# Gated cross-attention and mixture of experts on one core: the routing table built from four single-pass columns per tile instead of two fp32 ones

## The chip, the cores and the metric

One core of a Trainium2 chip runs the whole kernel in one launch. The metric is device time in microseconds (us), from the start to the end of the execution. TensorE does matrix products, VectorE, ScalarE and GpSimd work on rows of up to 128 partitions, SyncE issues DMAs. In rows of the profile PE is TensorE, PEld its weight loads, DVE is VectorE, ACT is ScalarE, POOL is GpSimd, SP is SyncE.

## The reference, cut to what matters

```python
x = x + tanh(g_xattn) * attention(layernorm(x), ctx)        # 32 heads, 8 groups, causal
xt = layernorm(x).reshape(2048, 512)                         # T = 2048 tokens
scores = softmax(xt @ Wg.T)                                  # E = 16 experts
masked = scores of the 2 best of 4 groups of experts, -inf elsewhere
topi = top_k(masked, 4);  weights = scores at topi
combine = zeros(T, E).at[token, topi].add(weights)
y = sum over experts e of (silu(xt @ W1[e].T) * (xt @ W3[e].T)) @ W2[e].T * combine[:, e]
z = (silu(xt @ Ws1.T) * (xt @ Ws3.T)) @ Ws2.T                # the shared expert
x = x + tanh(g_ffn) * (y + z)
```

## The kernel before, in words

`build` runs five stages: `stage_project`, `stage_attend`, `stage_close`, `stage_shared` and `stage_experts`. The change lies in `stage_shared` alone, which computes the shared expert and, woven into it, the routing. `stage_experts` follows and works through TILES = 79 tiles of 128 gathered rows, each of one expert.

**The shared expert.** The work is cut into 24 units, `units`, in the order b = 0 to 3 (512 tokens each) and, within b, n = 5, 0, 1, 2, 3, 4 (128 hidden columns each, the first only 64). A unit is 12 products for `gate` and 12 for `up` (`multiply`, L1405; unit n = 5 has only `gate`). Each is an fp32r product, that is one pass over fp32 words that hold a rounded value; three such passes over a high and a low part (`PASSES`) make up fp32. After the last unit of a b come 68 products into `yps` (`down`, L1417). Behind each unit ScalarE takes `act` and `upc` out of PSUM, GpSimd multiplies them into `raw` (L1378), ScalarE rounds that to the high part of `h` (L1340), and GpSimd subtracts it to get the low part (L1380). `gate` and `up` have two buffers each, so that TensorE in unit i waits for ScalarE's work on unit i - 2 (`s_act`, `s_upc`).

**Routing.** VectorE alone works out the softmax, the four experts of each token, and for each of the 2048 x 4 pairs of token and expert a slot in the list of 79 x 128 rows: `row` (slot mod 128) and `col` (slot div 128), for NT = 16 groups of 128 tokens and NK = 4 choices. Its small operations wait for each other by the semaphore `s_v`, one after the other. It waits once on TensorE for the counts (L1198).

**The table.** What the experts stage needs is the inverse: for each slot, which token is in it and at which scale. It is made as a sum of outer products. For each group t VectorE writes `at_row[t % 2]` (L1250: 1 where `row` equals the partition number, [128, 4, 128], 512 elements per partition), `at_tile` (L1254: 1 where `col` equals the tile number, [128, 4, 79], one buffer), and `at_col[t % 2]` (L1258, twice: `at_tile` times `put[..., 0]`, which is the token's number less T less `row`, and `at_tile` times `put[..., 1]`, the scale; [128, 4, 79] each). TensorE then runs `table(t)` (L1427): for each k one fp32 product of `at_row[:, k]` (128x128, as weights) and `at_col[:, k]` (158 columns), all 64 of them summed in the PSUM tile `tokps` [128, 158].

**The order around it.** TensorE runs its queue in order. After the products of unit i, for i = 8 to 15, it runs `table(2 * (i - 8))` and `table(2 * (i - 8) + 1)`, each behind a wait on `s_row` for VectorE's operations of that group. Units 8 to 11 are followed by the `down` products of b = 1, and units 12 to 15 are the first of b = 2 (unit 12 is the narrow one). VectorE, before it writes `at_row` of group t, waits on `s_tok` for `table(t - 2)`; nothing else holds it in this loop. After the tables VectorE turns `tokps` into `scatter`, `gather` and `scale` (L1284 to L1293). GpSimd waits for `gather` (`compared[1]`) before unit 20 of 24, where it issues the first four gathers, and the experts stage reads `scatter` and `scale`.

```python
for k in range(NK):
    mm = eng.matmul(tokps[:], at_row[r][:, k, :], at_col[r][:, k].rearrange("p n g -> p (n g)"), start=t == 0 and k == 0,
```

Of the kernel before, what the change touches and what calls it, by code (L numbers as in the profile page):

```python
# [9 lines left out]
F32 = mybir.dt.float32  # L10
F32R = mybir.dt.float32r
# [5 lines left out]
P = 128  # L17
BATCH, SEQ, D = 4, 512, 512
T = BATCH * SEQ
# [11 lines left out]
E, EG, TOPG, TOPK = 16, 4, 2, 4  # L31
# [4 lines left out]
NT = T // P  # L36
TILES = T * TOPK // P + E - 1
# [1021 lines left out]
def stage_shared(nc, io, dram, out):  # L1059

    with ExitStack() as c:  # L1061
        sb = lambda n, s, d=F32: c.enter_context(nc.sbuf_tensor(n, s, d))
        sem = dsem = lambda n: c.enter_context(nc.semaphore(n))

        NG, NK, SEAM = E // EG, TOPK, 24
        big = lambda n, d=F32: sb(n, [P, NT, E], d)
# [4 lines left out]
        top, topi, topf = sb("r_top", [P, NT, 8]), sb("r_topi", [P, NT, 8], mybir.dt.uint32), sb("r_topf", [P, NT, 8])  # L1071
# [8 lines left out]
        tok, slots = sb("r_tok", [P, NT]), sb("r_slots", [P, NT, NK], I32)  # L1080
# [3 lines left out]
        row, col = sb("r_row", [P, NT, NK]), sb("r_col", [P, NT, NK])  # L1084
        at_row = [io["rows"][2 + r].rearrange("p (k n) -> p k n", k=NK) for r in range(2)]
        at_tile = sb("r_attile", [P, NK, TILES])
        at_col = [sb(f"r_atcol{r}", [P, NK, 2, TILES]) for r in range(2)]
        put = sb("r_put", [P, NT, NK, 2])
        pad_i, pad = sb("r_padi", [P, 1], I32), sb("r_pad", [P, 1])
# [6 lines left out]
        within, totals = counts[:, 0], counts[:, 1]  # L1096
        tokps = ps("r_tokps", [P, 2 * TILES])
        s_c, s_i, s_exp, s_ch, s_mm, s_v = (
# [9 lines left out]
        x1 = [residual(io, b) for b in range(BATCH)]  # L1108
        gf, tg = sb("s_gf", [P, 1]), sb("s_tg", [P, 1])
        gate = [ps(f"s_gate{i}", [P, SEQ]) for i in range(2)]  # L1110
        up = [ps(f"s_up{i}", [P, SEQ]) for i in range(2)]
# [11 lines left out]
        def _(eng):  # L1123
            begin(eng, s_c, s_ch, s_v, s_row, s_tile, s_high, s_low)
            done = itertools.count(2)
            eng.wait_ge(s_i, 6)
            eng.tensor_copy(pad[:], pad_i[:]).then_inc(s_v, 1)
            eng.wait_ge(s_v, next(done))
            eng.tensor_copy(iota_e[:], iota_i[:]).then_inc(s_v, 1)
# [54 lines left out]
            eng.wait_ge(s_tg, 2)  # L1184
            eng.tensor_scalar(put[:, :, :, 1], top[:, :, 0:NK], tg[:, 0:1], None, ALU.mult).then_inc(s_v, 1)
            eng.wait_ge(s_v, next(done))
# [56 lines left out]
            eng.wait_ge(s_v, next(done))  # L1243
            eng.tensor_tensor(put[:, :, :, 0], rows(tok[:].rearrange("p (t o) -> p t o", o=1), NK), row[:], ALU.subtract).then_inc(s_v, 1)
            eng.wait_ge(s_v, next(done))
            for t in range(NT):
                r = t % 2
                if t >= 2:
                    eng.wait_ge(s_tok, t)
                eng.tensor_tensor(at_row[r], iota_p[:].rearrange("p (o n) -> p o n", o=1).broadcast_to([P, NK, P]),  # L1250
                                  row[:, t, :].rearrange("p (k o) -> p k o", o=1).broadcast_to([P, NK, P]), ALU.is_equal).then_inc(s_row, 1)
                if t:
                    eng.wait_ge(s_row, 3 * t + 1)
                eng.tensor_tensor(at_tile[:], iota_g[:].rearrange("p (o g) -> p o g", o=1).broadcast_to([P, NK, TILES]),  # L1254
                                  col[:, t, :].rearrange("p (k o) -> p k o", o=1).broadcast_to([P, NK, TILES]), ALU.is_equal).then_inc(s_tile, 1)
                eng.wait_ge(s_tile, t + 2)
                for n in range(2):
                    eng.tensor_tensor(at_col[r][:, :, n, :], at_tile[:],  # L1258
                                      put[:, t, :, n:n + 1].broadcast_to([P, NK, TILES]), ALU.mult).then_inc(s_row, 1)

# [23 lines left out]
            eng.tensor_scalar(indexf[:], tokps[:, 0:TILES], pad[:, 0:1], None, ALU.add).then_inc(s_v, 1)  # L1284
            eng.wait_ge(s_v, next(done))
            eng.tensor_copy(io["scatter"], indexf[:]).then_inc(s_v, 1)
            eng.wait_ge(s_v, next(done))
# [4 lines left out]
            eng.wait_ge(s_v, compared[1])  # L1292
            eng.tensor_copy(io["scale"], tokps[:, TILES:]).then_inc(s_v, 1)  # L1293
            eng.wait_ge(s_v, next(done))
# [57 lines left out]
        def _(eng):  # L1352
            begin(eng, s_i, s_xlow, s_raw, s_hlow, s_sum)
            eng.iota(iota_i[:], pattern=[[1, E]], base=0, channel_multiplier=0).then_inc(s_i, 1)
            eng.iota(tok_i[:], pattern=[[P, NT]], base=-T, channel_multiplier=1).then_inc(s_i, 1)
            eng.iota(iotag_i[:], pattern=[[1, TILES]], base=0, channel_multiplier=0).then_inc(s_i, 1)
# [32 lines left out]
        def _(eng):  # L1389
# [33 lines left out]
            def table(t):  # L1423
                r = t % 2
                eng.wait_ge(s_row, 3 * t + 4)
                for k in range(NK):
                    mm = eng.matmul(tokps[:], at_row[r][:, k, :], at_col[r][:, k].rearrange("p n g -> p (n g)"), start=t == 0 and k == 0,  # L1427
                                    stop=t == NT - 1 and k == NK - 1, skip_group_check=True)
                mm.then_inc(s_tok, 1)
# [386 lines left out]
```

## Time and profile before

| | |
|---|---|
| median of 3 runs | 1238.58 us |
| lowest, highest | 1228.62, 1242.21 us |
| the profiled execution, its own time | 1229.68 us |
| its span, first to last instruction | 1227.9 us |
| mean granted TensorE clock | 0.985 |
| busy: PE, PEld | 1190.7 us (97%), 917.2 us (75%) |
| busy: DVE, ACT, POOL | 631.8 us (51%), 576.0 us (47%), 618.1 us (50%) |

The profiled execution is near the lowest of the three runs. Its time is 1.8 us more than its span. The stage with the change runs from about 440 to 660 us of the span, the tables from 517 to 586 us. Start times in the rows are in us from the span's start. A line of a timeline with x12 at its end is 12 instructions in a row, with the time from the start of the first to the end of the last; the ends of matmuls overlap the next ones, so the distance between two starts is what one costs its engine.

### The profile page before, as it was taken

What the parts mean: (1) busy time and instruction counts of PE and PEld (TensorE: products, weight loads), DVE (VectorE), ACT (ScalarE), POOL (GpSimd) and SP (SyncE); (2) the same over time, 40 slices, a digit from 0 to 9 for tenths busy, and PEclk for the clock granted to TensorE, in tenths of its full rate; (3) what the DMA queues carried; (4) which work ended last, traced back from release to release, by engine and by line L of the source; (5) the groups of instructions that cost most, each with busy time, mean ns of one, the idle gap of its engine ahead of it and who ended that gap; (6) DMA issues with size and microseconds to landing.
All of it is one profiled execution on the core that took longest, in us unless ns stands there. A gap on an engine that the chain in (4) does not pass through costs nothing. (4 is left out here: it accounts for less than half of the span.)

```text
span 1227.9 us, 23555 instructions
## 1 busy us (share of the span) xinstructions
PE 1190.7 (97%) x7779; PEld 917.2 (75%) x7780; DVE 631.8 (51%) x1829; ACT 576.0 (47%) x989; POOL 618.1 (50%) x655
## 2 busy tenths in 40 slices
PE   7999999999988989999998999999999999999996
PEld 5564555555543468888887999999999999999995
DVE  5437999999947847865141233222423344442100
ACT  1221777777741333322332555555555555555553
POOL 5010333443332615635562766667666676666663
PEclk8999999999989989999999999999999999999998
DMA  9462544444449250110133546566565655656433
GB/s 351 150 192 99 155 127 124 133 128 129 147 132 256 85 206 32 38 38 32 52 123 114 116 101 146 142 147 146 147 144 122 169 146 147 147 147 144 73 69 43
DMA packets 74829, 157.73 MB, mean 128 GB/s; under 512 B 10836, under 2 KB 16468, under 8 KB 73608
## 3 DMA queue, kind: packets, MB, share of 16 engines
q1 hardware_dynamic: 53720, 106.96, 27.1%
q0 software_dynamic: 21040, 49.88, 19.8%
q8 instruction: 41, 0.67, 0.2%
q14 instruction: 28, 0.23, 0.1%
HBM read 101.88 MB, written 52.49 MB: 126 GB/s over the span
## 5 line engine op out<-in xcount | busy, mean ns | idle before, releaser
L1555 DVE CAST e_w<-e_w 128x480 fp32r<-128x480 f32 x135 | 71.5, 530 | 304.9 <-DMA e_w<-in_w2T 300.8
L670 DVE CUSTOM_DVE_ANT_0 a_mb<-a_mb,late 128x512 f32<-128x512 f32 (+1 forms) x480 | 217.3, 526 | 6.4 <-PE a_mb L712 4.6
L1711 PE MATMUL e_yps<-e_w,e_hT 128*128 x711 | 197.2, 404 | 0.9 <-ACT e_hT L1620 0.9
L656 ACT ACTIVATE a_at<-a_eb 128x1024 f32<-128x1024 f32 (+1 forms) x192 | 163.5, 870 | 38.3 <-PE a_eb L733 25.7
L1582 POOL DMA_INDIRECT out<-e_y,scatter x79 | 130.4, 1651 | 99.0 <-ACT e_y L1629 95.4
L576 POOL TENSOR_SCALAR_AFFINE_SELECT a_at<-a_at 128x256 f32<-128x256 f32 (+1 forms) x192 | 93.8, 489 | 171.0 <-ACT a_at L656 170.9
L1690 PE MATMUL e_up<-e_w,e_xT 128*128 x948 | 170.5, 329 | 0.0
L1690 PE MATMUL e_gate<-e_w,e_xT 128*128 x948 | 168.8, 327 | 1.0 <-issue 1.0
L1690 PEld LDWEIGHTS e_gate<-e_w,e_xT 128*128 128x128 f32 x948 | 156.8, 190 | 11.1 <-issue 6.3
L1690 PEld LDWEIGHTS e_up<-e_w,e_xT 128*128 128x128 f32 x948 | 149.7, 189 | 0.0
L1711 PEld LDWEIGHTS e_yps<-e_w,e_hT 128*128 128x128 f32 x711 | 128.1, 189 | 25.4 <-issue 1.2
L712 PE MATMUL a_mb<-a_k,a_q 49*128 49x512 f32 (+1 forms) x480 | 132.3, 372 | 0.8 <-PEq L245 0.8
L712 PEld LDWEIGHTS a_mb<-a_k,a_q 49*128 49x128 f32 x480 | 74.2, 184 | 65.5 <-DVE a_mx L670 39.1
L1587 POOL TENSOR_TENSOR e_hT<-e_hc,e_hT 128x384 fp32r<-128x384 f32 x78 | 83.2, 1066 | 44.5 <-ACT e_hc L1622 44.4
L1562 DVE TENSOR_TENSOR e_w<-e_w 128x480 fp32r<-128x480 f32 x135 | 101.1, 749 | 4.7
L756 PE MATMUL a_pv<-a_at,a_v 128*32 128x128 f32 (+1 forms) x1792 | 102.2, 327 | 0.2
L1600 POOL TENSOR_TENSOR e_h<-e_act,e_upc 128x352 f32<-128x352 f32 x79 | 76.3, 966 | 39.7 <-ACT e_upc L1640 39.5
L105 POOL DMA_INDIRECT e_x<-dx,gather x79 | 81.9, 1036 | 12.2 <-issue 2.4
L1616 ACT ACTIVATE e_xT<-e_xps 128x512 fp32r<-128x512 f32 x79 | 47.2, 597 | 81.6 <-PE e_xps L1681 75.4
L733 PE MATMUL a_eb<-a_q,a_k 50*128 50x512 f32 (+1 forms) x256 | 84.2, 420 | 0.1
L1636 ACT ACTIVATE e_act<-e_gate 128x352 f32<-128x352 f32 x79 | 36.8, 465 | 95.1 <-PE e_gate L1690 77.9
L1640 ACT ACTIVATE e_upc<-e_up 128x352 f32<-128x352 f32 x79 | 36.9, 467 | 79.1 <-PE e_up L1690 79.1
(259 smaller groups left out, 1858.3 us busy)
## 6 DMA issues: line engine op xcount, KB each, us to landing
e_w<-in_w13T SPq DMA_DIRECT2D x16, 1408.0 KB, 7.1
dq<-p_parts SPq DMA_DIRECT2D x32, 256.0 KB, 2.4
a_q<-dq SPq DMA_DIRECT2D x64, 128.0 KB
do<-a_o SPq DMA_DIRECT2D x32, 256.0 KB, 2.3
e_w<-in_w2T SPq DMA_DIRECT2D x16, 512.0 KB, 4.2
a_k<-dk SPq DMA_DIRECT2D x64, 98.0 KB
e_w<-in_ctxT SPq DMA_DIRECT2D x4, 1024.0 KB, 15.3
e_w<-in_x SPq DMA_DIRECT2D x4, 1024.0 KB, 13.7
```

What stands on the lines that cost most here:

```text
L105: eng.indirect_dma_start(out=io["rows"][n], out_offset=None, in_=dram["x2"], in_offset=bass.IndirectOffsetOnAxis(ap=io["gather"][:, g:g + ...
L576: eng.affine_select(out=square, in_=square, compare_op=ALU.is_ge, fill=0.0, base=0, pattern=[[0, 2 * len(js)], [1, P]], channel_multiplier ...
L656: eng.activation(to, scores, ACT.Exp, scale=0.25).then_inc(s_exp, 1)
L670: eng.tensor_tensor_reduce(out=b[:, 0:w], in0=b[:, 0:w], in1=io["late"][:, SEQ - w:SEQ], scale=1.0, scalar=3 * NEG, op0=ALU.add, op1=ALU.m ...
L712: mm = eng.matmul(b, q[r][rows, j, ch * P:(ch + 1) * P], k[r][rows, 0:b.shape[-1]], start=True, stop=True)
L733: return eng.matmul(eb[u % 2][:, t, n0:SEQ], keys, q[r][rows, js[0], n0:SEQ], start=True, stop=True)
L756: mm = eng.matmul(pv[32 * h:32 * h + 32, cols], v[of % NB][:, ch, :], at[of % 2][:, ch, 2 * j + t, cols], start=ch == 0 and n0 == 0, stop= ...
L1562: eng.tensor_tensor(w[rows, r, rest], w[rows, r, rest].bitcast(F32), w[rows, r, cols].bitcast(F32), ALU.subtract).then_inc(s_low, 1)
L1582: eng.indirect_dma_start(out=out, out_offset=bass.IndirectOffsetOnAxis(ap=io["scatter"][:, g:g + 1], axis=0), in_=y[n][:], in_offset=None, ...
L1587: eng.tensor_tensor(hT[r][:, 1], hc[:], hT[r][:, 0].bitcast(F32), ALU.subtract).then_inc(s_hlow, 1)
L1690: mm = eng.matmul(out[r][:], xT[r][:, mine, k, :], w[:, bass.ds(buf, 1), its * SIDE + at:its * SIDE + at + INTER].rearrange("p b n -> p (b ...
L1711: mm = eng.matmul(yps[:], hT[r][0:size, mine, n, :], w[0:size, bass.ds(buf, 1), its * SIDE + at:its * SIDE + at + D].rearrange("p b n -> p ...
```

## The change

The table's products become fp32r, one pass each. An fp32r value holds fewer bits than an fp32 one, so index and scale are cut into parts that fp32r holds: a whole number between -127 and 127 (`lane - row`: the token's number within its group less its row), the group's multiple of 128 (`tok`, now without the lane), the scale's rounded part (`high`), and what it leaves. `put` and `at_col` so have PARTS = 4 columns where they had 2, `tokps` has 316 columns, and a product has 316 columns in place of 158. The four are multiplied by one VectorE operation per group, over [128, 4, 4, 79] = 1264 elements per partition, in place of two of 316. Five operations on 64 elements stand where one stood (before the first `at_row`), one of one element per partition is added at the stage's start, and after the tables two additions of 79 elements put the parts together again. The wait counts on `s_row` follow (two increments a group where there were three). Nothing else moves; all queues keep their order.

```diff
@@ -1062,7 +1062,7 @@
         sb = lambda n, s, d=F32: c.enter_context(nc.sbuf_tensor(n, s, d))
         sem = dsem = lambda n: c.enter_context(nc.semaphore(n))
 
-        NG, NK, SEAM = E // EG, TOPK, 24
+        NG, NK, SEAM, PARTS = E // EG, TOPK, 24, 4
         big = lambda n, d=F32: sb(n, [P, NT, E], d)
         z, score, masked, sel = (big(f"r_{n}") for n in ("z", "score", "masked", "sel"))
         slot, prod = masked, sel
@@ -1082,10 +1082,8 @@
         iota_pi = iota_p[:].bitcast(I32)
         rowi, coli = sb("r_rowi", [P, NT, NK], I32), sb("r_coli", [P, NT, NK], I32)
         row, col = sb("r_row", [P, NT, NK]), sb("r_col", [P, NT, NK])
-        at_row = [io["rows"][2 + r].rearrange("p (k n) -> p k n", k=NK) for r in range(2)]
+        at_row = [io["rows"][2 + r].bitcast(F32R).rearrange("p (k n) -> p k n", k=NK) for r in range(2)]
         at_tile = sb("r_attile", [P, NK, TILES])
-        at_col = [sb(f"r_atcol{r}", [P, NK, 2, TILES]) for r in range(2)]
-        put = sb("r_put", [P, NT, NK, 2])
         pad_i, pad = sb("r_padi", [P, 1], I32), sb("r_pad", [P, 1])
         indexf = sb("r_indexf", [P, TILES])
         tile_e, tile_b = sb("r_tilee", [1, TILES]), sb("r_tileb", [1, TILES])
@@ -1094,7 +1092,7 @@
         ps = lambda n, s: c.enter_context(nc.psum_tensor(n, s, F32))
         counts = ps("r_counts", [P, 2, NT, E])
         within, totals = counts[:, 0], counts[:, 1]
-        tokps = ps("r_tokps", [P, 2 * TILES])
+        tokps = ps("r_tokps", [P, PARTS * TILES])
         s_c, s_i, s_exp, s_ch, s_mm, s_v = (
             sem(f"r_s{n}") for n in ("c", "i", "exp", "ch", "mm", "v"))
         ready, expert = sb("r_ready", [1, TILES], I32), sb("r_expert", [1, TILES], I32)
@@ -1107,6 +1105,9 @@
         part = [sb(f"s_part{i}", [P, D]) for i in range(2)]
         x1 = [residual(io, b) for b in range(BATCH)]
         gf, tg = sb("s_gf", [P, 1]), sb("s_tg", [P, 1])
+        at_col = [sb(f"r_atcol{r}", [P, NK, PARTS, TILES], F32R) for r in range(2)]
+        put, high = sb("r_put", [P, NT, NK, PARTS]), sb("r_high", [P, NT, NK], F32R)
+        lane, whole = sb("r_lane", [P, 1]), sb("r_whole", [P, NT, NK])
         gate = [ps(f"s_gate{i}", [P, SEQ]) for i in range(2)]
         up = [ps(f"s_up{i}", [P, SEQ]) for i in range(2)]
         yps = [ps(f"s_yps{i}", [P, D]) for i in range(2)]
@@ -1125,6 +1126,8 @@
             done = itertools.count(2)
             eng.wait_ge(s_i, 6)
             eng.tensor_copy(pad[:], pad_i[:]).then_inc(s_v, 1)
+            eng.wait_ge(s_v, next(done))
+            eng.tensor_scalar(lane[:], pad[:], float(T), None, ALU.subtract).then_inc(s_v, 1)
             eng.wait_ge(s_v, next(done))
             eng.tensor_copy(iota_e[:], iota_i[:]).then_inc(s_v, 1)
             eng.wait_ge(s_v, next(done))
@@ -1182,7 +1185,7 @@
             eng.tensor_copy(topf[:], topi[:]).then_inc(s_v, 1)
             eng.wait_ge(s_v, next(done))
             eng.wait_ge(s_tg, 2)
-            eng.tensor_scalar(put[:, :, :, 1], top[:, :, 0:NK], tg[:, 0:1], None, ALU.mult).then_inc(s_v, 1)
+            eng.tensor_scalar(whole[:], top[:, :, 0:NK], tg[:, 0:1], None, ALU.mult).then_inc(s_v, 1)
             eng.wait_ge(s_v, next(done))
             for k in range(NK):
                 eng.tensor_tensor(one[k], iota_e[:].rearrange("p (o e) -> p o e", o=1).broadcast_to([P, NT, E]),
@@ -1241,7 +1244,15 @@
             eng.wait_ge(s_v, next(done))
             eng.tensor_copy(col[:], coli[:]).then_inc(s_v, 1)
             eng.wait_ge(s_v, next(done))
-            eng.tensor_tensor(put[:, :, :, 0], rows(tok[:].rearrange("p (t o) -> p t o", o=1), NK), row[:], ALU.subtract).then_inc(s_v, 1)
+            eng.tensor_scalar(put[:, :, :, 0], row[:], lane[:, 0:1], -1.0, ALU.subtract, ALU.mult).then_inc(s_v, 1)
+            eng.wait_ge(s_v, next(done))
+            eng.tensor_copy(put[:, :, :, 1], rows(tok[:].rearrange("p (t o) -> p t o", o=1), NK)).then_inc(s_v, 1)
+            eng.wait_ge(s_v, next(done))
+            eng.tensor_copy(high[:], whole[:]).then_inc(s_v, 1)
+            eng.wait_ge(s_v, next(done))
+            eng.tensor_copy(put[:, :, :, 2], high[:].bitcast(F32)).then_inc(s_v, 1)
+            eng.wait_ge(s_v, next(done))
+            eng.tensor_tensor(put[:, :, :, 3], whole[:], high[:].bitcast(F32), ALU.subtract).then_inc(s_v, 1)
             eng.wait_ge(s_v, next(done))
             for t in range(NT):
                 r = t % 2
@@ -1250,13 +1261,12 @@
                 eng.tensor_tensor(at_row[r], iota_p[:].rearrange("p (o n) -> p o n", o=1).broadcast_to([P, NK, P]),
                                   row[:, t, :].rearrange("p (k o) -> p k o", o=1).broadcast_to([P, NK, P]), ALU.is_equal).then_inc(s_row, 1)
                 if t:
-                    eng.wait_ge(s_row, 3 * t + 1)
+                    eng.wait_ge(s_row, 2 * t + 1)
                 eng.tensor_tensor(at_tile[:], iota_g[:].rearrange("p (o g) -> p o g", o=1).broadcast_to([P, NK, TILES]),
                                   col[:, t, :].rearrange("p (k o) -> p k o", o=1).broadcast_to([P, NK, TILES]), ALU.is_equal).then_inc(s_tile, 1)
                 eng.wait_ge(s_tile, t + 2)
-                for n in range(2):
-                    eng.tensor_tensor(at_col[r][:, :, n, :], at_tile[:],
-                                      put[:, t, :, n:n + 1].broadcast_to([P, NK, TILES]), ALU.mult).then_inc(s_row, 1)
+                eng.tensor_tensor(at_col[r][:], at_tile[:].rearrange("p k (o g) -> p k o g", o=1).broadcast_to([P, NK, PARTS, TILES]),
+                                  put[:, t].rearrange("p k (n o) -> p k n o", o=1).broadcast_to([P, NK, PARTS, TILES]), ALU.mult).then_inc(s_row, 1)
 
             eng.wait_ge(io["s_xTout"][BATCH - 2], 32)
             eng.tensor_tensor(cmp, iota_g[0:1, :].rearrange("p (g o) -> p g o", o=1).broadcast_to([1, TILES, E]),
@@ -1283,6 +1293,8 @@
             eng.wait_ge(s_tok, NT + 1)
             eng.tensor_scalar(indexf[:], tokps[:, 0:TILES], pad[:, 0:1], None, ALU.add).then_inc(s_v, 1)
             eng.wait_ge(s_v, next(done))
+            eng.tensor_tensor(indexf[:], indexf[:], tokps[:, TILES:2 * TILES], ALU.add).then_inc(s_v, 1)
+            eng.wait_ge(s_v, next(done))
             eng.tensor_copy(io["scatter"], indexf[:]).then_inc(s_v, 1)
             eng.wait_ge(s_v, next(done))
             eng.tensor_scalar(indexf[:], indexf[:], float(T - 1), None, ALU.min).then_inc(s_v, 1)
@@ -1290,7 +1302,9 @@
             eng.tensor_copy(io["gather"], indexf[:]).then_inc(s_v, 1)
             compared.append(next(done))
             eng.wait_ge(s_v, compared[1])
-            eng.tensor_copy(io["scale"], tokps[:, TILES:]).then_inc(s_v, 1)
+            eng.tensor_copy(io["scale"], tokps[:, 2 * TILES:3 * TILES]).then_inc(s_v, 1)
+            eng.wait_ge(s_v, next(done))
+            eng.tensor_tensor(io["scale"], io["scale"], tokps[:, 3 * TILES:], ALU.add).then_inc(s_v, 1)
             eng.wait_ge(s_v, next(done))
 
             eng.wait_ge(io["s_w"], LOAD)
@@ -1352,7 +1366,7 @@
         def _(eng):
             begin(eng, s_i, s_xlow, s_raw, s_hlow, s_sum)
             eng.iota(iota_i[:], pattern=[[1, E]], base=0, channel_multiplier=0).then_inc(s_i, 1)
-            eng.iota(tok_i[:], pattern=[[P, NT]], base=-T, channel_multiplier=1).then_inc(s_i, 1)
+            eng.iota(tok_i[:], pattern=[[P, NT]], base=-T, channel_multiplier=0).then_inc(s_i, 1)
             eng.iota(iotag_i[:], pattern=[[1, TILES]], base=0, channel_multiplier=0).then_inc(s_i, 1)
             eng.iota(iota_pi, pattern=[[1, P]], base=0, channel_multiplier=0).then_inc(s_i, 1)
             eng.iota(pad_i[:], pattern=[[0, 1]], base=T, channel_multiplier=1).then_inc(s_i, 1)
@@ -1422,7 +1436,7 @@
 
             def table(t):
                 r = t % 2
-                eng.wait_ge(s_row, 3 * t + 4)
+                eng.wait_ge(s_row, 2 * t + 3)
                 for k in range(NK):
                     mm = eng.matmul(tokps[:], at_row[r][:, k, :], at_col[r][:, k].rearrange("p n g -> p (n g)"), start=t == 0 and k == 0,
                                     stop=t == NT - 1 and k == NK - 1, skip_group_check=True)
```

## Rows read from the trace of the kernel before

**Rows 1.** The page's first part, and the granted clock in 40 slices of the span
```profile
PE 1190.7 (97%) x7779; PEld 917.2 (75%) x7780; DVE 631.8 (51%) x1829; ACT 576.0 (47%) x989; POOL 618.1 (50%) x655
...
PEclk8999999999989989999999999999999999999998
```

**Rows 2.** Who TensorE waited for, 440 to 665 us: total, times, longest
```profile
PE s_gate L1405 <- issue: 1.5, 1, 1.5
PE e_xps L1674 <- POOL e_h L1590: 1.3, 1, 1.3
PE c_tp L1008 <- ACT e_w L895: 0.8, 1, 0.8
```

**Rows 3.** Busy time of each engine in stretches of the tables
```profile
core 0: us, PE busy (x) PEld busy (x) DVE busy (x) ACT busy (x) POOL busy (x), PEclk, DMA share, GB/s
505.00:542.00 37.00, 37.00 (x191) 32.02 (x189) 27.10 (x41) 10.96 (x18) 16.23 (x12) 1.00 0.07 22
558.00:586.00 28.00, 28.00 (x151) 24.57 (x149) 20.26 (x27) 8.13 (x14) 11.66 (x9) 1.00 0.08 29
```

**Rows 4.** Timeline of TensorE, one period of the tables and its neighbours
```profile
517.04 2.32 PE L1427 MATMUL r_tokps<-r_atcol,e_x 128*128 128x158 f32 x16
519.09 3.01 PE L1405 MATMUL s_gate<-s_xT,s_ws 128*128 x12
521.94 2.88 PE L1405 MATMUL s_up<-s_xT,s_ws 128*128 x12
524.66 2.32 PE L1427 MATMUL r_tokps<-r_atcol,e_x 128*128 128x158 f32 x16
```

**Rows 5.** Timeline of TensorE in the experts stage, products of 352 columns
```profile
673.98 1.91 PE e_up L1690 x12
```

**Rows 6.** Timeline of VectorE in the same period
```profile
518.32 1.48 DVE L1250 TENSOR_TENSOR e_x<-r_iotap,r_row 128x512 f32<-128x512 f32 x1 [3.57 <-PE r_tokps L1427]
519.72 0.47 DVE L1254 TENSOR_TENSOR r_attile<-r_iotag,r_col 128x316 f32<-128x316 f32 x1
520.23 1.86 DVE L1258 TENSOR_TENSOR r_atcol<-r_attile,r_put 128x316 f32<-128x316 f32 x2
522.01 0.68 DVE L1250 TENSOR_TENSOR e_x<-r_iotap,r_row 128x512 f32<-128x512 f32 x1
522.62 0.47 DVE L1254 TENSOR_TENSOR r_attile<-r_iotag,r_col 128x316 f32<-128x316 f32 x1
523.12 0.89 DVE L1258 TENSOR_TENSOR r_atcol<-r_attile,r_put 128x316 f32<-128x316 f32 x2
525.94 1.48 DVE L1250 TENSOR_TENSOR e_x<-r_iotap,r_row 128x512 f32<-128x512 f32 x1 [1.93 <-PE r_tokps L1427]
```

**Rows 7.** Timeline of GpSimd in the same period
```profile
517.98 1.27 POOL L1378 TENSOR_TENSOR s_raw<-s_act,s_upc 128x512 f32<-128x512 f32 x1 [1.94 <-ACT s_upc L1334]
520.00 1.35 POOL L1380 TENSOR_TENSOR s_h<-s_raw,s_h 128x512 fp32r<-128x512 f32 x1 [0.74 <-ACT s_h L1340]
525.60 1.27 POOL L1378 TENSOR_TENSOR s_raw<-s_act,s_upc 128x512 f32<-128x512 f32 x1 [4.25 <-ACT s_upc L1334]
```

**Rows 8.** VectorE: a product of 1264 elements, then a cast and a subtraction of 480
```profile
L1262 DVE TENSOR_TENSOR e_w<-r_iotag,r_base 1x1264 f32<-1x1264 f32 x1 | 1.5, 1457 | 0.0
...
627.29 0.41 DVE L1300 CAST e_w<-e_w 128x480 fp32r<-128x480 f32 x1
627.73 0.66 DVE L1302 TENSOR_TENSOR e_w<-e_w 128x480 fp32r<-128x480 f32 x1
```

**Rows 9.** How soon TensorE starts once what it waits for has ended
```profile
662.04 0.60 ACT L1614 ACTIVATE e_xT<-e_xps 128x512 fp32r<-128x512 f32 x1 [6.54 <-PE e_xps L1674]
...
662.70 0.49 PE L1681 MATMUL e_xps<-e_xT,k_lessr 128*128 128x512 f32 x1 [0.69 <-ACT e_xT L1614]
```

**Rows 10.** Timeline of VectorE: the wait for counts, the last small operation, the first groups
```profile
487.66 0.42 DVE L1198 COPY r_tot<-r_counts 128x256 f32<-128x256 f32 x1 [5.59 <-PE r_counts L1443]
...
507.39 0.23 DVE L1244 TENSOR_TENSOR r_put<-r_tok,r_row 128x64 f32<-128x64 f32 x1
...
512.89 1.86 DVE L1258 TENSOR_TENSOR r_atcol<-r_attile,r_put 128x316 f32<-128x316 f32 x2
```

**Rows 11.** After the tables: VectorE's last operation, and GpSimd's first gather
```profile
589.47 0.24 DVE L1293 COPY scale<-r_tokps 128x79 f32<-128x79 f32 x1
...
625.24 1.24 POOL L105 DMA_INDIRECT e_x<-dx,gather  x1 [0.16 <-issue]
```

## The prediction, made before the change was run

> **What bounds the kernel now.** I read the busy shares first, then who TensorE waited for in the stage with the change, then the timelines of the engines over one period of the tables. TensorE is busy for 97% of the span, VectorE and GpSimd for about half, and the granted clock is near full throughout [rows 1]. In the 225 us around this stage TensorE's longest wait is 1.5 us and none is at a table product [rows 2]; over both stretches with tables it is busy for the whole of 37.00 and 28.00 us, at a granted clock of 1.00, that is the 2.4 GHz level [rows 3]. So TensorE's own work sets the end here, and a microsecond less on it is a microsecond less at the end, as long as no wait takes its place. The reader is to see in TensorE's timeline that the period is 7.62 us (517.04 to 524.66): gate, up, and two tables [rows 4]. In VectorE's timeline the two groups for the next pair of tables are written from 518.32 to 524.01, so 0.65 us before TensorE comes back to the tables, and VectorE then idles 1.93 us until the next table frees its buffer [rows 6]. That margin is what the change draws on.
>
> **Part 1, the products.** From the first table product to the first gate product are 2.05 us for 8 fp32 products, recorded as 16 [rows 4]. The gate's 12 products then take 2.85 us to the start of up, and up's 12 take 2.72 us, that is 0.227 us each; the gate's 0.13 us more is paid at the turn from fp32. Two tables cost 2.18 us. One fp32r product of 316 columns has no row. From below there is 0.134 us, the distance of the fp32 records (0.134 from 2.14 over 16), from above 0.227 us for 512 columns [rows 4]. Nearest are 352 columns in 1.91 us for 12, 0.159 us [rows 5]. Through the two points (352, 0.159) and (512, 0.227) a column costs 0.425 ns, so 316 columns cost 0.144 us, which I take. Eight cost 1.15 us, with no turn between kinds. TensorE saves 2.18 - 1.15 = 1.03 us a pair, and 8.2 us over eight pairs, if it never waits. Its period would be 5.44 + 1.15 = 6.60 us. With 0.134 the saving is 8.9 us, with 0.227 it is 2.9 us.
>
> **Part 2, the operations per group.** Undisturbed, VectorE's group costs 0.61 us for `at_row`, 0.50 for `at_tile` and 0.89 for the two `at_col` to their end (522.01 to 524.01) [rows 6]. One operation over 1264 elements of two fp32 inputs, both of them broadcast, took 1.457 us, on one partition [rows 8]. I take 1.46 us: a group then needs 2.57 us to its end, 2.49 us to the start of the next, against 1.93. The bounds: from below 0.8 us, if it ran at the rate of the cast (0.41 us for 480 elements where two inputs take 0.66) [rows 8], as the new operation also writes fp32r; from above 1.96 us, four times the longest undisturbed single one (0.49 us at most, since 0.89 covers two), if the third level of the access pattern were paid as four starts [rows 6].
>
> **Part 3, GpSimd in the way.** The first group of the pair takes 3.69 us and the second 2.00, with the same work [rows 6]. `at_row` started at 518.32 while GpSimd's product ran from 517.98 to 519.25, and ended at 519.80, 0.55 us after it, where its 512 elements take about 0.53; the `at_col` pair from 520.23 is 0.97 us too long, and GpSimd's next operation ended at 521.35 [rows 6, 7]. The two engines exclude each other, and GpSimd has 2.62 us of this a period. This is what the Trainium skill says in "SBUF — State Buffer", section "Who interferes with whom": a VectorE instruction with two inputs in SBUF contends with a GpSimd instruction that reads SBUF, and whichever comes later is blocked to the other's end. The trace agrees, with the 1.48 against 0.68 us. By the rule the two sums must be added, 4.98 + 2.62 = 7.60 us against TensorE's 6.60; without it VectorE's 4.98 us would be hidden and the whole saving kept.
>
> I laid the schedule out with these durations, each operation blocked to the other's end and then taking its stream time (0.35 us for 316 elements, 0.55 for 512, 1.33 for 1264), and TensorE starting 0.10 us after its release (between 0.06, as 662.64 to 662.70 [rows 9], and 0.25 if the weight load is seen in full). Tables 0 and 1 run from 517.04 to 518.20. VectorE starts at 517.81, group 2 ends at 521.48 and group 3 at 525.12. TensorE comes to table 2 at 523.64 and to table 3 at 524.22, and waits 1.00 us for it. On the second refill groups 4 and 5 end at 529.76 and 532.24, TensorE is at table 5 at 531.82 and waits 0.52; on the third, group 7 ends at 539.47, TensorE is there at 538.93 and waits 0.64. Then the 16 us of down products hide the fourth refill whole. The second block (units 12 to 15) repeats it with 0.90, 0.52 and 0.64. Sum of new waits: 4.2 us. Behind each waiting table stand the next unit's gate and up, so each such wait is paid in full.
>
> **Part 4, the rest.** Five small operations for one (0.23 us each and 0.03 between) start the first group 1.0 us later, and `at_col` adds 0.57 us a group: group 1, which ended at 514.75, ends at 516.9 by plain addition, and near 516.1 by the schedule, where it meets less of GpSimd [rows 10]. TensorE is at table 0 at 517.04 and at table 1, which needs it, 0.58 us later [rows 4]: cost 0, with 0.7 us of cover by the later of the two; without that cover each 0.1 us would cost 0.1. The one-element operation at the start is covered by the 5.59 us wait for the counts [rows 10]. The two additions after the tables come before 591 us, and the first gather waits until 625.24 [rows 11]: cost 0, 34 us of cover. GpSimd can be held back up to 1.46 us by the longer operation, but it idles 4.25 us in a period [rows 7], and the low part of `h` is due only in the down products.
>
> **The sum.** 8.2 - 4.2 = 4.0 us less. The profiled execution took 1229.68 us, its span and 1.8 us around it; it would take 1225.7. It is 0.7% under the median of the runs, so the median goes from 1238.58 to 1234.6 us, a change of 0.3%. About 1% is what a measurement of this kernel can tell from no change.
>
> **The rivals.**
> *Everything is hidden, 8.2 us less (1230.4).* VectorE's operation would have to be much shorter than 1.46 us, or GpSimd not block it. For it: nothing but the fp32r output, whose cast is quick [rows 8]. Against: the subtraction of rows 8 writes fp32r too and is at full length, and the blocking is in every period.
> *The long operation takes over, slower by up to 2 us (1240.6).* Place: `at_col`, in the six refills that no down products cover. By the same schedule each 0.1 us above 1.46 costs about 1.1 to 1.3 us, since it comes twice in each refill; the saving is eaten at 1.81 us, and at the bound of 1.96 the kernel is 2.0 us slower. For it: the output and inputs have one more level than the row of 1457 ns. Against: the two of 316 have that broadcast too and stay at one rate.
> *The product costs more than its columns.* At 0.227 us (as 512 columns) the saving is 2.9 us before the waits, some of which then vanish: 2.2 us less (1236.4). If the chip still made two passes of 316 columns each, which would be the change not doing what it says, a pair would cost 16 x 0.267 = 4.3 us, 2.1 more than now, and the kernel would be 17 us slower (1255.6). Against it: gate and up have fp32r on both sides and leave one record a product [rows 4].
>
> **How the numbers follow.** The forecast 0.58; all hidden 0.14; the long operation takes over 0.14; the dearer product 0.08; two passes 0.02; others, a wait further on among them, 0.04. The effects between -8.3 and +2.0 us on the median give 1230.3 to 1240.6. The three runs lie from 10 below to 4 above their median, and a new median can fall elsewhere among such runs; for this I widen to 1224 and keep 1241 above, since the likeliest effects are below zero. No mechanism but the two passes moves it by 12 us. Faster by over 1%: 0.04; within: 0.92; slower: 0.04, the two passes and a drift of the runs.
>
> **What would show it.** Right: L1427 with 64 records at distances of 0.144 us and granted clock 1.00; `at_col` at 1.46 us undisturbed and up to 2.6 disturbed; new waits of TensorE on VectorE at the second table of a pair, six of them, 4.2 us in all; pairs of unequal periods around 7.3 us in place of 7.62; the down products of b = 1 starting 1.8 us earlier than 541.95. Wrong: no waits at L1427 (then 8.2 us are gained), 128 records, `at_col` over 1.8 us, or waits of TensorE on ScalarE or GpSimd in units 9 to 17, which I have at none.

## The result, and the profile after

Over 14 runs of each kernel the median went from 1230.56 us (1227.07 to 1242.21) to 1224.87 us (1221.69 to 1233.09). The ratio is 0.9944, with a 95% interval of 0.9917 to 0.9971: 0.56% faster, and the interval excludes no change. The profiled execution took 1225.17 us, against 1229.68 before and 1225.7 as forecast for it.

The changed kernel's page has, against [rows 1], 8.6 us less of TensorE and 12.5 us more of VectorE:

```profile
PE 1182.1 (97%) x7715; PEld 906.6 (74%) x7716; DVE 644.3 (53%) x1820; ACT 576.1 (47%) x989; POOL 621.6 (51%) x655
...
PEclk8999999999988999999999999999999999999999
```

Who TensorE waited for in the same stretch as [rows 2], 440 to 665 us. The first line is new: seven waits of tables on `at_col`.

```profile
PE r_tokps L1441 <- DVE r_atcol L1268: 2.5, 7, 0.7
PE c_tp L1008 <- ACT e_w L895: 1.9, 2, 1.1
PE s_gate L1419 <- issue: 1.4, 1, 1.4
```

TensorE's timeline, the period that answers to [rows 4] and the next turn:

```profile
517.07 0.74 PE L1441 MATMUL r_tokps<-r_atcol,e_x 128*128 128x316 f32 x4
518.16 0.84 PE L1441 MATMUL r_tokps<-r_atcol,e_x 128*128 128x316 f32 x4 [0.34 <-DVE r_atcol L1268]
518.84 2.92 PE L1419 MATMUL s_gate<-s_xT,s_ws 128*128 x12
521.60 2.88 PE L1419 MATMUL s_up<-s_xT,s_ws 128*128 x12
524.32 0.74 PE L1441 MATMUL r_tokps<-r_atcol,e_x 128*128 128x316 f32 x4
525.37 0.85 PE L1441 MATMUL r_tokps<-r_atcol,e_x 128*128 128x316 f32 x4 [0.30 <-DVE r_atcol L1268]
526.05 2.93 PE L1419 MATMUL s_gate<-s_xT,s_ws 128*128 x12
```

The period is 7.25 us where it was 7.62 and where 6.60 was to be had. One table of four products takes 0.58 us without a wait. Here 1.09 and 1.05 us pass from the start of the first table of a pair to that of the second, so the second starts 0.5 us late.

VectorE's timeline over the first refill and the one before it, answering to [rows 6] and [rows 10], and then GpSimd's, answering to [rows 7]:

```profile
507.77 1.35 DVE L1249 COPY r_put<-r_tok 128x64 f32<-128x64 f32 x1
...
509.94 1.67 DVE L1261 TENSOR_TENSOR e_x<-r_iotap,r_row 128x512 fp32r<-128x512 f32 x1
...
515.65 2.45 DVE L1268 TENSOR_TENSOR r_atcol<-r_attile,r_put 128x1264 fp32r<-128x1264 f32 x1
518.02 0.68 DVE L1261 TENSOR_TENSOR e_x<-r_iotap,r_row 128x512 fp32r<-128x512 f32 x1
518.63 1.57 DVE L1265 TENSOR_TENSOR r_attile<-r_iotag,r_col 128x316 f32<-128x316 f32 x1
520.23 1.48 DVE L1268 TENSOR_TENSOR r_atcol<-r_attile,r_put 128x1264 fp32r<-128x1264 f32 x1
521.62 1.78 DVE L1261 TENSOR_TENSOR e_x<-r_iotap,r_row 128x512 fp32r<-128x512 f32 x1
523.33 0.47 DVE L1265 TENSOR_TENSOR r_attile<-r_iotag,r_col 128x316 f32<-128x316 f32 x1
523.84 1.48 DVE L1268 TENSOR_TENSOR r_atcol<-r_attile,r_put 128x1264 fp32r<-128x1264 f32 x1
```

```profile
518.01 1.84 POOL L1392 TENSOR_TENSOR s_raw<-s_act,s_upc 128x512 f32<-128x512 f32 x1 [1.25 <-ACT s_upc L1348]
520.59 2.26 POOL L1394 TENSOR_TENSOR s_h<-s_raw,s_h 128x512 fp32r<-128x512 f32 x1 [0.74 <-ACT s_h L1354]
```

VectorE no longer idles between refills, but for 12.9 us during the `down` products of b = 1. GpSimd's subtraction began at 520.59, inside `at_col` (520.23 to 521.70), and took 2.26 us where it took 1.35; VectorE's next `at_row`, at 521.62, then took 1.78 where it takes 0.68. Each waits until the other's operation has ended.

As a measure that leaves out the rest of the kernel I use the table stretch: from the first table product to the gate product behind the last table. It was 68.62 us (517.04 to 585.66) and is 64.97 (517.07 to 582.04), 3.65 us less. From the first table product to the start of the last product of the shared stage it was 141.23 us and is 137.21, so 4.0 us less: 3.65 in the stretch and 0.37 behind it. Of the 0.37, 0.27 us lie in the `down` products of b = 2 and b = 3, which the change does not touch: one of them costs 0.229 us in both traces of the kernel before and 0.227 in the others. Why is open.

### The profile page after: what moved, and what is told of

Its sections match the earlier page's. It is cut to its first block and busy times, and to the rows that moved or that the text cites. A ratio compares the mean times of both kernels' runs of the same rounds, so it can differ in the third digit from the quotient of the medians.

```text
span 1223.3 us, 23418 instructions
## 1 busy us (share of the span) xinstructions
PE 1182.1 (97%) x7715; PEld 906.6 (74%) x7716; DVE 644.3 (53%) x1820; ACT 576.1 (47%) x989; POOL 621.6 (51%) x655
## 5 line engine op out<-in xcount | busy, mean ns | idle before, releaser
L1601 POOL TENSOR_TENSOR e_hT<-e_hc,e_hT 128x384 fp32r<-128x384 f32 x78 | 80.7, 1034 | 46.0 <-ACT e_hc L1636 46.0
```

Source lines behind the costliest of these rows:

```text
L1601: eng.tensor_tensor(hT[r][:, 1], hc[:], hT[r][:, 0].bitcast(F32), ALU.subtract).then_inc(s_hlow, 1)
```

## The experiments

Single times of a kernel scatter by several us, so the experiments are read by their stretches in the trace, and totals only where they were timed in rounds.

**The product's part alone.** VectorE writes one of four columns; this leaves out all scales.

```diff
-eng.tensor_tensor(at_col[r][:], at_tile[:]..., put[:, t]..., ALU.mult)
+eng.tensor_tensor(at_col[r][:, :, 0, :], at_tile[:], put[:, t, :, 0:1].broadcast_to([P, NK, TILES]), ALU.mult)
```

> The product's part alone: VectorE writes one of the four columns per tile (316 elements, the whole index in one part), the other three are zeroed once, so all scales are left out (zero). TensorE still multiplies 316 columns in fp32r. The measure is the table stretch, from the first table product to the gate product behind the last table: 68.62 us before, 64.97 after. Theory A (the four-column operation makes VectorE too slow for the shorter period, and all of the lost gain is TensorE's wait for it): no waits at the tables, eight pairs at about 1.16 us in place of 2.18, stretch 60.5 to 60.8 us. Rival (the gain was lost on TensorE itself, by products that cost more than their columns or by a turn between kinds): stretch stays over 62 us with no wait recorded.

Measured: stretch 60.45 us, no wait. Its timeline of TensorE, one pair:

```profile
521.53 1.32 PE L1444 MATMUL r_tokps<-r_atcol,e_x 128*128 128x316 f32 x8
522.70 2.88 PE L1422 MATMUL s_gate<-s_xT,s_ws 128*128 x12
525.41 2.88 PE L1422 MATMUL s_up<-s_xT,s_ws 128*128 x12
528.13 1.32 PE L1444 MATMUL r_tokps<-r_atcol,e_x 128*128 128x316 f32 x8
```

The period is 6.60 us. The products are worth 8.17 us (68.62 - 60.45); the changed kernel gives back 4.52 of them (64.97 - 60.45). The rival falls: no part of the loss is in the products.

**VectorE's part alone.** The four parts as in the changed kernel, the product as before, on the first two columns; the scales are left out.

```diff
-mm = eng.matmul(tokps[:], at_row[r][:, k, :], at_col[r][:, k]...)          # fp32r
+mm = eng.matmul(tokps[:, 0:2 * TILES], at_row[r][:, k, :], at_col[r][:, k, 0:2]...)   # fp32
```

> VectorE's part alone: the four parts are written as in the changed kernel, but as fp32, and TensorE multiplies the two index columns only, as before in fp32 (158 columns); the scales are left out (they get index values). Theory A: TensorE's period of 7.62 us just holds two groups of 2.49 us and GpSimd's 2.6, so there is at most one wait, of about 0.1 us at the second table, and the stretch is 68.6 to 69.0 us, as before. Rival (the longer operation costs by itself, however long the period): the waits of the changed kernel appear here too, stretch 71 us or more.

Measured: stretch 68.48 us, and the profile lists no wait at a table. Two of the eight pairs take 2.14 and 2.11 us where the others take 2.03 to 2.05, which is about the 0.1 us expected. So the long operation costs nothing beyond that while the period is 7.62 us: only the shorter period and the longer operation together make the waits.

**GpSimd out of the way.** Its two operations of units 8 to 15 cover 64 of 512 columns; the other columns are left out.

```diff
+w = 64 if NS + 2 <= i < NS + 10 else SEQ
-eng.tensor_tensor(raw[i % 2][0:size], act[i % 2][0:size], upc[i % 2][0:size], ALU.mult)
+eng.tensor_tensor(raw[i % 2][0:size, 0:w], act[i % 2][0:size, 0:w], upc[i % 2][0:size, 0:w], ALU.mult)
```

> The changed kernel with GpSimd's two operations of units 8 to 15 cut from 512 to 64 columns (the product with up and the low part are left out for the other 448 columns of these units). Theory A (VectorE and GpSimd exclude each other, so their times add: 4.98 + 2.62 against TensorE's 6.60): with GpSimd down to some 0.3 to 0.5 us a period all waits behind the first pair are gone, stretch about 61 to 61.5 us. Rival B (GpSimd only shifts VectorE a little; the length of at_col and the hand-over set the wait): the waits stay, about 0.4 us at each second table, stretch 64 us or more.

Measured: stretch 61.09 us. Only the wait at table 1 is left, and it costs 0.64 us (61.09 - 60.45). Its timeline of VectorE:

```profile
515.60 0.68 DVE L1261 TENSOR_TENSOR e_x<-r_iotap,r_row 128x512 fp32r<-128x512 f32 x1
516.21 0.60 DVE L1265 TENSOR_TENSOR r_attile<-r_iotag,r_col 128x316 f32<-128x316 f32 x1
516.84 1.48 DVE L1268 TENSOR_TENSOR r_atcol<-r_attile,r_put 128x1264 fp32r<-128x1264 f32 x1
518.23 0.81 DVE L1261 TENSOR_TENSOR e_x<-r_iotap,r_row 128x512 fp32r<-128x512 f32 x1
...
522.70 0.69 DVE L1261 TENSOR_TENSOR e_x<-r_iotap,r_row 128x512 fp32r<-128x512 f32 x1 [1.74 <-PE r_tokps L1442]
```

`at_col` is as long as ever, and VectorE idles 1.74 us again. The waits come from the two engines' excluding each other; rival B falls.

**One wait taken away by itself.** Four small operations go ahead of the wait for the counts.

```diff
 eng.tensor_tensor(chosen[:], sel[:], one[3], ALU.add).then_inc(s_ch, 1)
+# the four that write put[..., 1], high, put[..., 2] and put[..., 3], from behind col
 eng.wait_ge(s_mm, 3)
```

> The changed kernel with the four small operations that make the parts (they need no slots) issued before VectorE's wait for the counts, where it idles 5.6 us. The first group starts over 1 us earlier. Theory A: the wait at table 1 (0.49 us) is gone, but it had given VectorE time for groups 2 and 3, so the wait at table 3 grows from 0.46 to about 0.95 us and the stretch hardly moves: 64.6 us against 64.97. Rival (each wait is its own, as a sum of separate terms): 0.49 us less, stretch 64.5 us with all later waits unchanged at 0.4 to 0.5 us. What tells them apart is the wait at table 3.

Measured: stretch 64.69 us. Its timeline of TensorE:

```profile
515.73 1.32 PE L1441 MATMUL r_tokps<-r_atcol,e_x 128*128 128x316 f32 x8
...
522.33 0.74 PE L1441 MATMUL r_tokps<-r_atcol,e_x 128*128 128x316 f32 x4
523.88 0.85 PE L1441 MATMUL r_tokps<-r_atcol,e_x 128*128 128x316 f32 x4 [0.80 <-DVE r_atcol L1268]
```

The wait at table 1 is gone and most of it comes back at table 3: 1.55 us from the start of one table to that of the next, where the changed kernel has 1.05 (524.32 to 525.37). Where VectorE is behind, taking away the first wait is worth 0.28 us (64.97 - 64.69), not the 0.64 that it costs where it is the only one.

**The tables spread.** One or two in each of units 8 to 18.

```diff
-if NS + 2 <= i < NS + 2 + NT // 2:
-    for t in range(2 * (i - NS - 2), 2 * (i - NS - 2) + 2):
+# {8: (0,), 9: (1, 2), 10: (3,), 11: (4, 5), 12: (6, 7), 13: (8,), 14: (9, 10), 15: (11,), 16: (12, 13), 17: (14,), 18: (15,)}
+    for t in TABLES.get(i, ()):
         table(t)
```

> The changed kernel with the 16 tables spread over units 8 to 18 (1, 2, 1, 2, then 2 after the down products, 1, 2, 1, 2, 1, then 1) in place of two in each of units 8 to 15. Measure: from the first table product to the last product of the shared stage, 141.23 us before, 137.21 after, 132.63 with the one-column operation. Theory A (VectorE and GpSimd together need 7.2 us for a pair of groups, which TensorE's 6.6 us does not cover, while 1.5 groups in 6 us fit): every wait at the tables goes, 132.6 to 133.4 us, and the kernel is about 4 us faster than the changed one, 0.992 to 0.995 of the kernel before by this part alone. Rival (VectorE falls behind as a whole, so spreading only moves the waits): 135 us or more, with waits at later units.

Measured: 132.91 us to the last product, no wait at a table, and 0.9914 (0.9882 to 0.9946) of the kernel before. VectorE has the time, only not in every unit.

**Four operations for one.**

```diff
-eng.tensor_tensor(at_col[r][:], ...)                                    # 1264 elements
+for n in range(PARTS):
+    eng.tensor_tensor(at_col[r][:, :, n, :], at_tile[:], put[:, t, :, n:n + 1].broadcast_to([P, NK, TILES]), ALU.mult)
```

> The changed kernel with at_col written by four operations of 316 elements in place of one of 1264. Theory A: each start costs about 0.08 us more than the stream, so a group is 0.25 us longer (4 x 0.41 to the next start, against 1.39), VectorE is on TensorE's path in six refills and this comes twice in each: the table stretch goes from 64.97 to about 67 us, near the 68.62 of the kernel before. Rival (GpSimd's operations slip in between the short ones and are done sooner, which pays for the starts): 65.0 us or less.

Measured: stretch 75.14 us, 8 us over what I expected. VectorE's row for the four is 0.20 us over the 1.48 of the one, about as expected:

```profile
524.55 1.68 DVE L1269 TENSOR_TENSOR r_atcol<-r_attile,r_put 128x316 fp32r<-128x316 f32 x4
```

TensorE's timeline and, in three stretches of it, busy time and granted clock (the last three columns: clock, DMA share, GB/s):

```profile
519.80 0.74 PE L1442 MATMUL r_tokps<-r_atcol,e_x 128*128 128x316 f32 x4
522.48 0.85 PE L1442 MATMUL r_tokps<-r_atcol,e_x 128*128 128x316 f32 x4 [1.93 <-DVE r_atcol L1269]
523.16 4.51 PE L1420 MATMUL s_gate<-s_xT,s_ws 128*128 x12
527.51 2.91 PE L1420 MATMUL s_up<-s_xT,s_ws 128*128 x12
530.26 1.32 PE L1442 MATMUL r_tokps<-r_atcol,e_x 128*128 128x316 f32 x8
...
594.26 0.84 PE L1442 MATMUL r_tokps<-r_atcol,e_x 128*128 128x316 f32 x4 [2.29 <-DVE r_atcol L1269]
594.94 4.50 PE L1420 MATMUL s_gate<-s_xT,s_ws 128*128 x12
```

```profile
517.00:523.00 6.00, 4.07 (x21) 3.31 (x20) 5.96 (x10) 2.93 (x5) 3.27 (x3) 1.00 0.00 0
523.16:527.51 4.35, 4.35 (x14) 3.40 (x13) 4.28 (x8) 0.00 (x0) 1.01 (x1) 0.61 0.00 0
527.51:530.26 2.75, 2.75 (x13) 2.25 (x12) 1.44 (x4) 0.60 (x1) 0.00 (x0) 1.00 0.00 0
```

A wait of 1.93 us was followed by a gate of 4.35 us in place of 2.72, at a granted clock of 0.61, which is a stretch mostly at the 1.2 GHz level. That came four times, behind each of its four waits (1.9 to 2.3 us). The fourth such gate starts where the stretch ends, so three of them count: 3 x 1.62 = 4.9 of the 8 us. The other 3.2 us are waits: they cost 9.7 us in all, counted from TensorE's starts, where the 67 us expected leave 6.5. No run separates why they are so long. Nowhere in the table stretch of the changed kernel did the clock fall, with waits up to 0.66 us. Both theories missed this; the rival, which had no loss, falls.

**Three parts.** The index in one column, as a whole number from -2175 to -1, and the scale in two.

```diff
-NG, NK, SEAM, PARTS = E // EG, TOPK, 24, 4
+NG, NK, SEAM, PARTS = E // EG, TOPK, 24, 3        # and 3 * TILES + 1 = 238 columns
-eng.tensor_scalar(put[:, :, :, 0], row[:], lane[:, 0:1], -1.0, ALU.subtract, ALU.mult)
+eng.tensor_tensor(put[:, :, :, 0], rows(tok[:]..., NK), row[:], ALU.subtract)
```

> Three parts in place of four: the index (a whole number from -2175 to -1) in one column as in the kernel before, scale high and low in two; the product has 238 columns, one of them zero, and at_col 948 elements. Theory A (a product costs by its columns, 0.11 us for 238; VectorE's group is 0.33 us shorter): stretch 60.5 to 61.5 us, waits gone but perhaps one of under 0.3 us at the first pair. Rival (four columns were made because a product of fewer columns leaves the single-pass rate): a product costs 0.2 us or more, and the stretch is 64 us or more, without waits. Should the index not be held exactly in one part, the output would differ.

Measured: stretch 61.01 us; a product takes 0.11 us (eight from 514.89 to 515.80), so it costs by its columns at 238 too, and one fp32r part carries the index: it need not have been cut in two. The stretch is 4.0 us shorter than the changed kernel's, but from two sources. The narrower products save 2.0 us by themselves (a pair takes 0.91 us in place of 1.16, eight times), and only 1.9 us are waits gone. Four waits are left, 1.0 us by the profile, and 2.6 us are still lost (61.01 against 60.45 - 2.0). TensorE's timeline:

```profile
514.89 1.07 PE L1441 MATMUL r_tokps<-r_atcol,e_x 128*128 128x238 f32 x8
515.80 2.92 PE L1419 MATMUL s_gate<-s_xT,s_ws 128*128 x12
```

**All three together, twice.**

> All that promises something together: three parts, the tables spread over units 8 to 18, and the operations that need no slots ahead of the wait for the counts. From the first table product to the last product of the shared stage: by theory A 132.6 us less 64 x 0.035 for the narrower products, 130.4 us, against 137.21 in the changed kernel; so 6.8 us faster than that and 10.8 us faster than the kernel before in this part, a ratio of about 0.991 if the rest of the kernel stays. Rival: products of 238 columns at 0.2 us or more, 136 us or more.

> The version with three parts, spread tables and early operations once more, unchanged. From the first table product to the last product of the shared stage 131.0 us again (137.2 in the changed kernel), and if the changed kernel stands at 0.994 to 0.997 of the kernel before, this one stands about 0.005 lower, near 0.991.

Measured: 130.98 us to the last product in both (130.4 expected), no wait at a table, and 0.9917 (0.9877 to 0.9957), then 0.9931 (0.9900 to 0.9961) of the kernel before. It beats both kernels: it takes 10.25 us off the stage where the change takes 4.0, and in the comparison in which the changed kernel ran beside it (further down) the medians are 1220.64 against 1227.64 us. Against the tables spread alone the whole-kernel comparison shows no difference; the stage does, by 1.9 us, about what the narrower products save.

**The size of the whole.** The first tile of the experts stage differed between the two traces, at a place the change does not touch. I ran both kernels again.

> The kernel before once more, unchanged. The question is the first tile of the experts stage: its first 12 gate products to the first of the next tile took 7.63 us in the kernel before, at a granted clock of 0.5 for some 4 us, and 6.10 us in the changed one at 1.0. Theory C (chance, or where the stage falls in time, as 7.4 to 8.7 us were also seen with one column, with VectorE alone, with four operations and with the best version, and 6.1 with four others): it may come out at 6.1 here as well; the table stretch is 68.6 us whatever it does. Rival D (the change itself takes the slow clock away there): 7.6 us or more again.

> The changed kernel once more, unchanged, on the same chip as the version below. The table stretch is 64.9 to 65.0 us again, with seven waits. Theory C: the first tile may take 7.6 us or more this time, and runs of the kernel spread over 10 us as before. Rival D: 6.1 us again. Against the kernel before 0.994 to 0.997.

Measured: the kernel before had 68.62 us of stretch and 7.63 us of first tile again; the changed one had 64.90 and, this time, 7.72. One row of each trace over the start of that stage, the first trace of the changed kernel, then the second:

```profile
660.00:662.00 2.00, 2.00 (x13) 2.00 (x14) 0.00 (x0) 0.00 (x0) 0.00 (x0) 1.00 1.01 407
```

```profile
654.00:660.00 6.00, 4.67 (x18) 4.29 (x18) 0.00 (x0) 1.66 (x3) 0.00 (x0) 0.72 0.87 309
```

Of the 14 traces of this study 9 have the slow clock there, of both kernels, and the first tile then takes 7.4 to 8.7 us, and 6.1 otherwise. Rival D falls: the 1.5 us were not the change's. The ratio came out at 0.9989 (0.9964 to 1.0015), lower in gain than either theory had it, so I ran the comparison a third time.

> The changed kernel a third time, for the size of the whole effect: two comparisons gave 0.9944 and 0.9989, which don't agree well, while the traces put the table stretch 3.65 and 3.72 us shorter and the stage 4.0 to 4.1 us. If the change does only what the stretch shows, the ratio lies at 0.9965 to 0.997, between the two, and slow clocks that come and go outside the stretch make up the rest. Rival: the change has a second effect outside the stage (0.9944 holds), or gives its gain back later in the kernel (0.9989 holds).

Measured: stretch 64.90 us, first tile 7.66, ratio 0.9942 (0.9915 to 0.9969). So the third agrees with the first. By their means the three comparisons give 6.2, 3.2 and 8.0 us. Put together, 36 runs of the changed kernel have a median of 1225.0 us and 50 of the one before 1230.5, 5.5 us apart, and their means lie 5.7 apart with a standard error of 0.9. The stage explains 4.0 to 4.1 us. The 1.5 us between are within two standard errors; whether a second effect of that size exists stays open. Much of the scatter comes ahead of the tables: the first table product starts anywhere from 511.34 to 522.84 us in the 14 traces, and in the three traces of the changed kernel at 511.34, 513.19 and 517.07 us.

## Why the prediction was right or wrong

**Wrong: the base, and what can be told.** I forecast a change of 0.3%, one that could not be told from none, and 1234.6 us. The runs showed 0.56% less, an interval clear of no change, and 1224.87 us. The step that failed is the last of "The sum": carrying 4.0 us onto 1238.58 us, and holding that against a limit of 1%. The median lies near the lower end of my range (1224 to 1241), and by luck: the effects alone gave 1230.3 to 1240.6, and only the widening for scatter reaches it. That median was of three runs that lay 14 us apart; 14 runs gave 1230.56, and the profiled execution was nearer to it. From 1230.56 the same sum gives 1226.6. I had written that the profiled one lay 0.7% under the median, and kept the median all the same. And the 1% that I gave as what can be told came from three runs; 14 runs of each gave an interval of 0.3% to either side. Of the 5.7 us measured, the stage explains the 4.0 forecast; the rest is open, as said above. That the profiled execution came within 0.5 us of 1225.7 is luck too: 1.5 us of its gain are the first tile of the experts stage, and the kernel from the second tile on took 0.9 us longer.

**The products: right.** 0.144 us forecast; 64 records of the changed kernel, 0.146 us apart where none waits (0.58 for four), 8.17 us saved where 8.2 was forecast, shown by the run with one column.

**The long operation: right.** 1.48 us against 1.46. The rival in which it takes over has no ground: at this length it costs nothing by itself.

**The exclusion, and the waits: right in kind, near in size.** Forecast 4.2 us in six waits; measured 4.52 us in seven. The run with the early operations has the six waits of the forecast and loses 4.24 us (64.69 - 60.45); so the sum was right, and the seventh wait belongs to part 4. The profile's waits sum to only 2.5 us, for two reasons: the row counts from the modelled end of the last product, 0.16 us after the next could have started (starts are 0.146 us apart and each is drawn 0.31 us long), and behind a wait the first product leaves 0.25 us to the second in place of 0.146. Over seven waits these are 1.1 and 0.7 us. That the exclusion makes the waits is shown by the run with GpSimd shortened, where all but the first are gone. The periods are 7.25, 7.22 and 7.19 us in the first block and 7.53 and 7.09 in the second, where I had "around 7.3". That is under the 7.60 of my plain addition, which is an upper bound here.

**The 4.0 us of the stage: the right size, partly by luck.** The forecast was 8.2 - 4.2, all of it at the tables. Measured there: 8.17 - 4.52 = 3.65 us. What brings the stage to 4.02 is mostly the 0.27 us in the `down` products of b = 2 and b = 3, for which I had no term; those of b = 1, inside the stretch, have 0.13 us more of it.

**Part 4: wrong in one term.** I gave the five small operations and the two first groups a cost of 0 with 0.7 us of cover. VectorE reached the first `at_row` at 509.94, 2.3 us later than before and not 1.0: the copy into `put` (L1249) met GpSimd and took 1.35 us where 0.23 was assumed, and `at_row` and `at_col` of these groups met it again (1.67 and 2.45 us). I had counted small operations at their undisturbed rate in an engine that is disturbed. By the run with the early operations, the waiting of table 1 that came of it cost 0.28 us.

**The rivals.** "Everything is hidden" was right as a price: the one-column run has it. The dearer product falls with the 0.146 us, and "two passes" is excluded by the 64 records.

**The rest** held: no waits of TensorE on ScalarE or GpSimd in units 9 to 17; down products of b = 1 at 540.47, 1.5 us earlier, where 1.8 was forecast.

## What to carry to other kernels

Where two engines exclude each other, add their busy times per period and hold the sum against the period that the change would leave, not the one that it has. Each part of this change by itself was free or full gain, and only together did they lose half. The sum is an upper bound (7.60 us here, 7.1 to 7.5 measured). If the sum doesn't fit, spread the consumer's work over periods or drop a part, rather than remove single waits, which come back at the next. And put a forecast difference on a base of many runs; the median of three was 8 us off.

## What the runs showed of the hardware that I had not expected

A wait has a second price. Behind each of four waits of a table, of 1.9 to 2.3 us, the granted clock fell to its lower level for some 3 to 4 us, and 12 products took 4.35 us instead of 2.72; behind waits of a table of up to 0.80 us it stayed at 1.00. So a wait of 1.93 us took 3.6 us from TensorE. Part of it came back, as VectorE went on meanwhile and the next pair of tables had no wait (530.26, eight products in a row). A change that makes waits longer can still lose more than their sum. That TensorE's clock can fall again and again from waits inside a loop is also what the Trainium skill says ("TensorE: Matmul & The Clock Gate", section "HAM oscillation — how this bites in real kernels"); the four gates above agree.

The same program, run again, had the low clock at the start of the experts stage or not (6.10 and 7.72 us for one tile), with the same waits ahead of it (1.38, 0.69 and 0.64 us). With one trace of each kernel this looks like a gain of the change.

VectorE's copy of 64 elements (L1249), with one input, was held by GpSimd: it started at 507.77, GpSimd's product ended at 509.03, and it took 1.35 us. I had looked for this only at operations with two inputs. The Trainium skill has it ("SBUF — State Buffer", section "Who interferes with whom": copies, casts and operations with a scalar can take the shared ports too), and the trace agrees.
